# v and the heads' results kept in DRAM in a two-stage attention kernel, their projections done a tile at a time

## The chip, the cores and the metric

One NeuronCore of a Trainium2 chip runs the kernel. The metric is the device time of one execution in microseconds; lower is better. The core has four engines that compute and that wait for each other through semaphores: TensorE (PE) for matmuls, VectorE (DVE), ScalarE (ACT) and GpSimd (POOL). A fifth, SyncE (SP), issues the DMA transfers of this kernel in order. Each engine works through its own instructions strictly in the order in which they stand.

## What is computed

x is [8, 1024, 512], the context [8, 1024, 384], all float32. Two layers follow each other, each with a gate tanh(g) and a residual:

```
x = x + tanh(g0) * xattn(layernorm(x), ctx)
x = x + tanh(g1) * ffn(layernorm(x))

xattn: q = x Wq, k = ctx Wk, v = ctx Wv            (8 heads of 64)
       out = softmax(q k^T / sqrt(64)) v Wo + bo
ffn:   q, k, v = x W^T + b                          (16 heads of 32)
       q = (q / |q| + emb) * softplus(temp)
       h = softmax(q k^T / sqrt(32)) v
       gates = softmax over 15 routed (top 3 kept, times 3) and over 2 shared logits of h
       out = (h * sum of gates) Wp^T + bp
```

Where the projections need more than one rounded product they are made of two parts: a tensor is split into a rounded half (hi) and the rest (lo), and three products hi*hi, hi*lo, lo*hi are added.

## The kernel before, in words

The kernel runs two stages, first the cross attention of all eight batches, then the second attention of all eight. A batch is a *turn* of 64 *steps*. A step T takes 128 keys against 512 queries for one *group* of G heads that fill 128 channels (G is 2 in the first stage and 4 in the second). Eight steps make a *half*: all 1,024 keys for 512 queries. Two halves are a group, four groups a turn.

Each piece of work is an item with a short name: S the scores of one head in a step (line 963), ex its exponential on ACT (line 1168), ad the adding up of exponentials over a half on POOL (line 856), PV the weighing of v (line 978), sm the sums over partitions by a matmul with ones (line 990), sma their reciprocal on ACT, ev the normalizing multiply on DVE (lines 1352 to 1355). Exponentials lie in a ring of 7 (first stage) or 10 buffers (second); a step that is the first of a half writes to buffers of its own, onto which POOL adds the others. In the second stage POOL adds six of the eight steps of a half, four heads each.

For the next group, pq and pk project queries and keys, sd copies them six times a head into the operand stack (line 765), mx and mxr find the maxima (lines 945 and 1327), mt, ml and md put them there too (line 780). In the second stage ss, ssa, s2, s3 and s3p normalize the queries (lines 921, 1109 to 1123, 1309 to 1311, 843).

Around the change: vp is the value projection of one 128-row tile (8 tiles in a batch, 9 matmuls each in the first stage, 12 in the second); vpe copies it into v inside the SBUF tensor vh, which holds v of a whole batch (lines 1135 and 1319). cp copies the accumulator of a half out of PSUM into the same tensor (line 1173), over parts of v that are used up. When all heads of a batch are done, hs and hsl split a tile of 128 rows (lines 1196 and 1345), op is its output projection with 12 matmuls, xb and ope add bias, gate and residual, st stores it. gt makes the gates' logits of a tile (line 999) and gm the gates of four tiles (from line 1362). Because v and results share vh, the value projection of a batch stands in that batch's first steps, right after the output projection of the batch before.

What stands when is decided by class Plan before anything is recorded. Every item has an engine, a duration, a due step (numbers in the table AT) and items that it waits for. `run` plays them in time: each engine takes the ready item with the earliest due step. The outcome is one list, and every engine records its items in that list's order:

```
self.add(("vp", TT * j + t, k), "pe", 0.69, b0 + t - 0.4 + 0.4 * k / whole, ...)
self.add(("op", t, k), "pe", 0.69, b + 0.2 + 0.1 * k, ...)
for it in sorted(line, key=lambda x: (step[x], str(x))):
```

PSUM has eight banks. A unit of work takes one of them when it begins (mx takes four) and frees it when its taker has read it.

## Time and profile before

| | us |
|---|---|
| median of 3 runs | 5062.16 (5056.38 to 5085.25) |
| the profiled execution, time | 5047.21 |
| its span | 5045.4 |
| PE busy | 4586.3 |
| POOL busy | 3357.6 |
| DVE busy | 2949.3 |
| ACT busy | 2596.8 |

Busy time is the union of an engine's instructions. A matmul's end is modelled and matmuls overlap, so the pace of PE is better read from one start to the next. The time of an execution lies 2 us above the span of its instructions.

### The profile page before, as it was taken

Reading aid. Unit: us, or ns where it says so; the run is one execution under the profiler, and the core shown is the slowest. Engines: PE = TensorE matmul, PEld = TensorE weight load, DVE = VectorE, ACT = ScalarE, POOL = GpSimd, SP = SyncE. Lnnn points to the kernel's source line nnn. Section 1 sums busy time; section 2 is a strip of 40 time slices with the busy share of each in tenths; the row PEclk is TensorE's granted clock in tenths of the full one; section 3 lists DMA queues with packets and bytes.
Section 4 is the critical chain, followed back from the end, with each engine's and each line's share of the span. In section 5 each row is a group of like instructions: output and inputs, shape, how many; then the busy total and the mean of one; then the engine's idle time right before and its main releaser. Section 6 shows DMA issues by size and latency. Waiting matters only on the chain.

```text
span 5045.4 us, 66897 instructions
## 1 busy us (share of the span) xinstructions
PE 4586.3 (91%) x21568; PEld 2358.1 (47%) x21568; DVE 2949.3 (58%) x3955; ACT 2596.8 (51%) x4705; POOL 3357.6 (67%) x2667
## 2 busy tenths in 40 slices
PE   4999999999999999988988888988888988989988
PEld 3554555555555555453444444543543533534534
DVE  5464646464545464656656656656656666666562
ACT  3445444444444444546646546556456466466464
POOL 2656566666666565648768668678478578578597
PEclk8999999999999999999999899999899999999998
DMA  7344444353434343322332222313213222232320
GB/s 240 101 136 114 125 123 126 119 132 120 109 121 109 119 111 113 89 94 70 86 88 59 76 84 59 105 55 84 84 51 84 84 68 68 84 84 60 101 51 26
DMA packets 285207, 481.06 MB, mean 95 GB/s; under 512 B 32832, under 2 KB 165440, under 8 KB 275648
## 3 DMA queue, kind: packets, MB, share of 16 engines
q1 hardware_dynamic: 284864, 476.79, 34.5%
q8 instruction: 178, 2.92, 0.3%
q14 instruction: 165, 1.35, 0.1%
HBM read 223.14 MB, written 50.33 MB: 54 GB/s over the span
## 4 chain that ended last, share of the span: by engine, by line
PE 38%; issue 8%; ACT 5%; POOL 4%; DVE 4%; DMA 2%; SPq 0%; ACTq 0%; POOLq 0%; DVEq 0%
PE aux L877 13%; PE aux L978 9%; PE aux L963 8%; POOL added_f L856 4%; PE aux L945 3%; ACT probs L1168 2%; PE aux L990 2%; DVE nm L1327 1%; DMA xs<-x_after_xattn 1%; PE aux L999 1%; PE aux L921 1%; ACT more L1168 1%; DMA out<-xs 1%; DVE halves_f L1345 1%; DVE st L1263 1%
## 5 line engine op out<-in xcount | busy, mean ns | idle before, releaser
L856 POOL TENSOR_TENSOR added<-added,probs 128x512 f32<-128x512 f32 x1433 | 1802.5, 1291 | 921.6 <-PE aux L978 657.1
L1327 DVE TENSOR_REDUCE nm<-aux 128x2 f32<-128x1024 f32 x1536 | 1810.4, 1220 | 791.4 <-PE aux L945 789.5
L1168 ACT ACTIVATE probs<-aux 128x512 f32<-128x512 f32 x2151 | 1190.5, 600 | 904.8 <-PE aux L963 837.3
L963 PE MATMUL aux<-stack 128*128 128x512 f32 x4096 | 1426.0, 440 | 127.7 <-ACT probs L1168 78.7
L963 PEld LDWEIGHTS aux<-stack 128*128 128x128 f32 x4096 | 711.6, 192 | 973.7 <-issue 365.1
L978 PE MATMUL aux<-probs,vh 128*32 128x512 f32 (+1 forms) x4302 | 991.0, 632 | 66.2 <-ACT vh L1135 21.0
L856 POOL TENSOR_TENSOR added_f<-added_f,probs 128x512 f32<-128x512 f32 x537 | 677.4, 1295 | 184.0 <-PE aux L978 131.1
L945 PE MATMUL aux<-ck_hi,cq_hi 32*128 32x512 f32 (+1 forms) x3072 | 460.8, 492 | 158.2 <-DVE nm L1327 109.4
L877 PE MATMUL aux<-xT_hi,wqk 128*128 128x512 f32 x1536 | 583.2, 416 | 4.1 <-DVE xT_lo L1290 2.0
L945 PEld LDWEIGHTS aux<-ck_hi,cq_hi 32*128 32x128 f32 (+1 forms) x3072 | 182.9, 188 | 633.1 <-issue 618.2
L1168 ACT ACTIVATE more<-aux 128x512 f32<-128x512 f32 x537 | 302.3, 602 | 149.9 <-PE aux L963 111.0
L877 PEld LDWEIGHTS aux<-xT_hi,wqk 128*128 128x128 f32 x1536 | 293.9, 191 | 129.1 <-issue 67.1
L856 POOL TENSOR_TENSOR added_f<-added_f,more 128x512 f32<-128x512 f32 x231 | 292.7, 1293 | 51.7 <-PE aux L978 26.0
L856 POOL TENSOR_TENSOR added<-added,more 128x512 f32<-128x512 f32 x231 | 290.2, 1283 | 47.3 <-PE aux L978 39.9
L978 PEld LDWEIGHTS aux<-probs,vh 128*32 128x32 f32 (+1 forms) x4302 | 157.9, 120 | 347.4 <-issue 206.5
L978 PE MATMUL aux<-more,vh 128*32 128x512 f32 x1074 | 301.3, 640 | 12.9 <-ACT probs L1168 11.6
L877 PE MATMUL aux<-xT_lo,wqk 128*128 128x512 f32 x768 | 305.6, 398 | 0.0
L1352 DVE SCALAR_TENSOR_TENSOR aux<-aux,rn 128x512 f32<-128x512 f32 x128 | 88.9, 695 | 356.4 <-ACT rn L1181 200.0
L1168 ACT ACTIVATE added<-aux 128x512 f32<-128x512 f32 x256 | 145.2, 599 | 153.5 <-PE aux L963 152.6
L877 PE MATMUL aux<-wvo,halves_f 128*128 128x512 f32 x768 | 212.6, 427 | 0.0
L862 POOL TENSOR_TENSOR xs<-xs,bo_x 128x512 f32<-128x512 f32 x64 | 82.4, 1303 | 193.4 <-DMA xs<-in_x 193.3
L877 PE MATMUL aux<-wvo,halves_x 128*128 128x512 f32 x768 | 192.7, 398 | 2.0 <-DVE nm L1327 1.4
(132 smaller groups left out, 4800.9 us busy)
## 6 DMA issues: line engine op xcount, KB each, us to landing
wqk<-w_split SPq DMA_DIRECT2D x256, 256.0 KB, 3.8
wvo<-w_split SPq DMA_DIRECT2D x64, 1024.0 KB, 6.9
stack<-cq_hi SPq DMA_DIRECT2D x128, 256.0 KB, 5.1
stack<-ck_hi SPq DMA_DIRECT2D x128, 256.0 KB, 5.0
stack<-cq_hi SPq DMA_DIRECT2D x256, 128.0 KB, 2.3
stack<-ck_hi SPq DMA_DIRECT2D x256, 128.0 KB, 2.4
xs<-in_x SPq DMA_DIRECT2D x16, 1024.0 KB, 6.7
stack<-cq_lo SPq DMA_DIRECT2D x64, 256.0 KB, 4.9
```

Of the source, the lines that this page charges most:

```text
L856: pool.tensor_tensor(onto, onto, exp_buffer(T, e), ALU.add).then_inc(added_ok, 1)
L862: pool.tensor_tensor(xs[:, t % (TT // 2), :], xs[:, t % (TT // 2), :], bo[:], ALU.add).then_inc(biased, 1)
L877: ins = pe.matmul(out, lhs(a, k), rhs(c, k), start=k == 0 and i == 0, stop=k == whole - 1 and i == 2)
L921: done(it, pe.matmul(out, blk[:], sq[:, n], start=True, stop=True))
L945: ins = pe.matmul(aux[:, b, :], cq["hi"][r, t * P:(t + 1) * P], ck["hi"][r, half * HALF:(half + 1) * HALF], start=True, stop=True)
L963: ins = pe.matmul(out, stack[:, g % 2, e * ph.SLOTS + ks, jt * P:(jt + 1) * P], stack[:, g % 2, e * ph.SLOTS + qs, n * HALF:(n + 1) * HALF ...
L978: ins = pe.matmul(out[e * D:(e + 1) * D, :], v[:, g, jt * P + e * D:jt * P + (e + 1) * D], exp_buffer(T, e), start=jt == 0, stop=jt == TT - 1)
L990: ins = pe.matmul(out[e * D:(e + 1) * D, :], ones[:, 0:ph.SUM], exp_buffer(T, e), start=i == 0, stop=i == ph.APART)
L999: ins = pe.matmul(out[:, i * GC:(i + 1) * GC], outputs(t)[:, k, :], wg[:, k, :], start=k == 0, stop=k == NG - 1)
L1168: act.activation(exp_buffer(T, e), aux[:, o.bank["S", T, e], :], ACT.Exp, scale=ph.SCALE).then_inc(probs_ok, 1)
L1327: dve.tensor_reduce(nm[:, half, first:first + 2 * TT - t:TT], aux[:, b:b + 2, :], axis=AX.X, op=ALU.max, negate=True).then_inc(emptied["dv ...
L1352: link(dve.scalar_tensor_tensor(src, src, -1.0, rn[:], ALU.mult, ALU.mult))
```

## The change

v and the results of the heads no longer lie in SBUF for a whole batch. A tile of v goes from v_out to v_kept in DRAM (item vs), and a group's 128 channels of v come back before the group's first step (vl), into one of two buffers. After each half ev multiplies straight out of the accumulator's PSUM bank into h_raw (cp is gone), hs and hsl split that half, and hw stores both parts to h_kept. ol loads the two parts of one tile of 128 rows with all channels, into one of two buffers, for op. So the value projection of a batch can be done in the turn before it, and its output projection in the turn after it. In the second stage gt and ga add the gates' logits group by group into an SBUF tensor glog, and gm works there. The table AT has new numbers, the durations of the items are changed a little, POOL's adds are items of one head each, and `run` adds 0.1 to a PE item where the split of the array changes or PE was idle. The context comes in three loads of one chunk instead of two.

```diff
-AT = (dict(p=[2.5, 16.43, 38.3, 52.31], over=6.61, mx0=-7.25, mxn=10.51, ctx=[-6.39, 14.17, 26.21, 32.42], load=[12.79, 23.3], norm=[17.14, 36.41], turned=[20.42, 27.54], out=[62.76, 53.38], xr=40.63, split=37.96, off={"gt": 0.84, "ope": 1.44, "mxr": -0.41, "pkl": -3.12, "s3": -1.53, "s2": 0.03, "pqa": 1.84}),
-      dict(p=[1.88, 20.24, 30.77, 50.7], over=6.36, mx0=-4.19, mxn=11.61, load=[-5.48, 6.89], norm=[5.16, 26.23], turned=[24.2, 36.67], out=[61.26, 62.43], xr=52.33, off={"cp": -2.01, "hsl": -0.72, "s2": 0.05, "gt": -0.98, "s3": -0.06, "ev": 1.12, "PV": -0.81}))
+AT = (dict(p=[2.5, 18.6, 35.2, 51.9], over=7.4, mx0=-6, mxn=9, ctx=[19, 24, 29], load=[25, 32], norm=[28.5, 34.5], turned=[30.5, 37],
+           vp=[38, 3], out=[1.5, 3], xr=-8, split=42, off={}),
+      dict(p=[2, 18.6, 36, 50], over=6.5, mx0=-5.5, mxn=9, load=[25, 32], norm=[28.5, 34.5], turned=[30.5, 37],
+           vp=[39, 3], out=[1.5, 3], xr=-8, off={}))
...
-            if ph.is_added(T):
-                self.add(("ad", T), "pool", 1.3 * G, T, [("ex", T, 0), ("ad", T - 1), ("PV", T - T % TT)])
+                self.add(("ex", T, e), "act", 0.48, T - 1 + 0.2 * e, after)
+                if ph.is_added(T):
+                    self.add(("ad", T, e), "pool", 1.24, T + 0.2 * e, [("ex", T, e), ("ad", T, e - 1), ("ad", T - 1, e), ("PV", T - T % TT)])
             after = [("ex", T, G - 1), ("PV", T - 1)]
-            if T % TURN < TT:
-                after += [("vpe", TT * j + T % TURN)]
-            self.add(("PV", T), "pe", 1.05, T + 0.9, after)
+            after += [("vl", T // STEPS)]
+            self.add(("PV", T), "pe", 0.86, T + 0.9, after)
             if jt == TT - 1:
-                b = T + 1 + ph.AT.get("sums", 0)
-                self.add(("cp", h), "act", 0.6, T + 0.95, [("PV", T), ("cp", h - 1)])
-                self.add(("sm", h), "pe", 0.9 * (1 + ph.APART), b, [("ad", T - ph.APART), ("ex", T, G - 1), ("sm", h - 1)])
-                self.add(("sma", h), "act", 1.3, b + 0.3, [("sm", h), ("ev", h - 1)])
-                self.add(("ev", h), "dve", 2.2, b + 0.6, [("sma", h), ("cp", h), ("ev", h - 1)])
+                b = T + 1
+                self.add(("sm", h), "pe", 0.86 * (1 + ph.APART), b, [("ad", T - ph.APART, G - 1), ("ex", T, G - 1), ("sm", h - 1)])
+                self.add(("sma", h), "act", 1.2, b + 0.3, [("sm", h), ("ev", h - 1)])
+                self.add(("ev", h), "dve", 2.07, b + 0.6, [("sma", h), ("PV", T), ("ev", h - 1), ("hw", h - 1)])
+                if ph.ffn:
+                    self.add(("gt", h), "pe", 0.45, b + 1, [("ev", h), ("fb", 0)])
+                    self.add(("ga", h), "dve", 0.2, b + 1.2, [("gt", h), ("gm", 2 * (h // HALVES - 1) + h % 2)])
+                self.add(("hs", h), "act", 0.55, b + 1, [("ev", h)])
+                self.add(("hsl", h), "dve", 0.6, b + 1.2, [("hs", h), ("gt", h)])
+                self.add(("hw", h), "sp", 1.3, b + 1.5, [("hsl", h)])
...
     def values(self, j):
...
-        ph, b0 = stage(j), TURN * j
+
+        ph, b0 = stage(j), TURN * (j - 1)
         whole = ph.chunks("vp")
-        source = [("trl", j, n, NG - 1) for n in range(2)] if ph.ffn else [("cxl", j, ph.KC - 1)]
-        freed = [(kind, TT * j - 1) for kind in ("hsl", "gt")] + ([("ws", w) for w in range(4)] if j == 0 else [])
-        self.add(("wv", j), "sp", 1.3, b0 - 2, [("op", TT * j - 1, NG - 1), ("ws", ph.W + 2)])
-        for t in range(TT):
+        freed = [("ws", w) for w in range(4)] if j == 0 else []
+        before = ("op", TT * (j - 1) - 1, NG - 1) if j > 1 else ("vp", TT - 1, whole - 1)
+        self.add(("wv", j), "sp", 1.3, b0 + ph.AT["vp"][0] - 4, [before] * (j > 0) + [("ws", ph.W + 2)] + [("fs", 4 * NG - 1)] * ph.ffn)
+        for i in range(TT):
+            t, b = TT * j + i, b0 + ph.AT["vp"][0] + i * ph.AT["vp"][1]
+            source = [("trl", j, i // (TT // 2), NG - 1)] if ph.ffn else [("cxl", j, ph.KC - 1)]
             for k in range(whole):
-                self.add(("vp", TT * j + t, k), "pe", 0.69, b0 + t - 0.4 + 0.4 * k / whole, [("vp", TT * j + t, k - 1)] if k else [("wv", j)] + source + freed)
-            self.add(("vpe", TT * j + t), "dve" if ph.ffn else "act", 0.7, b0 + t, [("vp", TT * j + t, whole - 1)] + freed + ([("fb", 0)] if ph.ffn else []))
-        self.add(("wo", j), "sp", 1.3, b0 + TT, [("vp", TT * j + TT - 1, whole - 1), ("ws", ph.W + 3)])
+                self.add(("vp", t, k), "pe", 0.685, b + 0.4 * k / whole, [("vp", t, k - 1)] if k else [("wv", j), ("vp", t - 1, whole - 1)] + source)
+            self.add(("vpe", t), "dve" if ph.ffn else "act", 0.6, b + 0.5, [("vp", t, whole - 1), ("vs", t - 1)] + freed + [("fb", 0)] * ph.ffn)
+            self.add(("vs", t), "sp", 0.65, b + 0.7, [("vpe", t)])
+        for g in range(NG * j, NG * (j + 1)):
+            self.add(("vl", g), "sp", 0.65, (g - 1) * STEPS + 0.5, [("vs", TT * j + TT - 1), ("PV", (g - 1) * STEPS - 1), ("vl", g - 1)])
 
     def finish(self, j):
 
-        ph, at, b0 = stage(j), stage(j).AT, TURN * j
-        slots = NSPLIT[ph.ffn]
+        ph, at, b0 = stage(j), stage(j).AT, TURN * (j + 1)
+        whole = stage(j + 1).chunks("vp")
+        last = [("vp", TT * (j + 2) - 1, whole - 1)] if j + 1 < 2 * B else [("op", TT * j - 1, NG - 1)]
+        self.add(("wo", j), "sp", 1.3, b0 + at["out"][0] - 4, last + [("ws", ph.W + 3)])
         self.add(("xr", j), "sp", 2.6, b0 + at["xr"], [("tr", j + 1, 1, NG - 1), ("st", TT * j - 1), ("fs", NG * j + NG - 1)])
+        if ph.ffn:
+            for half in range(2):
+                self.add(("gm", 2 * j + half), "dve", 4, b0 + (2 if half else -4), [("ga", HALVES * (j + 1) - 2 + half), ("ope", TT * j - 1)])
...
+            self.add(("ol", t), "sp", 0.65, b - 1, [("hw", HALVES * (j + 1) - 2 + half), ("op", t - 2, NG - 1)])
             for k in range(NG):
-                self.add(("op", t, k), "pe", 0.69, b + 0.2 + 0.1 * k, [("op", t, k - 1)] if k else [("hsl", t), ("wo", j), ("xb", t), ("op", t - 1, NG - 1)])
-            self.add(("ope", t), "dve", 0.8, b + 0.6, [("op", t, NG - 1), ("xb", t)] + ([("gm", 2 * j + half)] if ph.ffn else []))
+                self.add(("op", t, k), "pe", 0.685, b + 0.1 * k, [("op", t, k - 1)] if k else [("ol", t), ("wo", j), ("op", t - 1, NG - 1)])
+            self.add(("ope", t), "dve", 0.66, b + 0.6, [("op", t, NG - 1), ("xb", t)] + [("gm", 2 * j + half)] * ph.ffn)
...
+        h_raw = sb("h_raw", [P, HALF])
+        h_hi = sb("h_hi", [P, HALF], F32R)
+        v_out = sb("v_out", [P, DM])
+        v = sb("v", [P, 2, TT, P])
+        parts = sb("parts", [P, 2, 2, NG, P], F32R)
...
+        v_kept = nc.dram_tensor("v_kept", [2, NG, P, TT, P], F32).ap()
+        h_kept = nc.dram_tensor("h_kept", [2, TT, P, 2, NG, P], F32).ap()
...
+                    elif kind == "vs":
+                        j, t = divmod(g, TT)
+
+                        wait_emptied(sp, ("vp", g))
+                        if j >= 2 and t == 0:
+
+                            for i in range(2):
+                                sp.wait_ge(v_loaded[i], 16 * (NG // 2) * (j - 1))
+                        sp.dma_start(v_kept[j % 2, :, :, t, :].rearrange("g p c -> p g c"), v_out[:].rearrange("p (g c) -> p g c", g=NG)).then_inc(v_stored, 16)
+                    elif kind == "vl":
+                        j = g // NG
+
+                        sp.wait_ge(v_stored, 16 * TT * (j + 1))
+                        if g >= 2:
+
+                            sp.wait_ge(weighed, (g - 1) * STEPS)
+                        sp.dma_start(v[:, g % 2], v_kept[j % 2, g % NG]).then_inc(v_loaded[g % 2], 16)
+                    elif kind == "hw":
+                        j, h = divmod(g, HALVES)
+
+                        sp.wait_ge(h_lo_ok, g + 1)
+                        if j >= 2 and h < 2:
+
+                            for i in range(2):
+                                sp.wait_ge(h_loaded[i], 16 * (TT // 2) * (j - 1))
+                        for part, done in enumerate((h_hi[:].bitcast(F32), h_raw[:])):
+                            sp.dma_start(h_kept[j % 2, h % 2 * TT // 2:(h % 2 + 1) * TT // 2, :, part, h // 2, :].rearrange("t p c -> p t c"),
+                                         done.rearrange("p (t c) -> p t c", c=P)).then_inc(h_stored, 16)
+                    elif kind == "ol":
+                        j, t = divmod(g, TT)
+
+                        sp.wait_ge(h_stored, 32 * (HALVES * (j + 1) - 1 + t // (TT // 2)))
+                        if g >= 2:
+
+                            wait_full(sp, ("op", g - 2))
+                        sp.dma_start(parts[:, g % 2].bitcast(F32), h_kept[j % 2, t]).then_inc(h_loaded[g % 2], 16)
...
 
                         pe.wait_ge(probs_ok, ph.scores(T, G - 1))
-                        if T % TURN < TT:
-
-                            wait_emptied(pe, ("vp", T // TURN * TT + jt))
+                        if T % STEPS == 0:
+
+                            pe.wait_ge(v_loaded[T // STEPS % 2], 16 * (T // STEPS // 2 + 1))
                         out = bank(it)
                         for e in range(G):
...
-                            pe.wait_ge(h_lo_ok, t + 1)
-                        ins = product(bank(it), lambda a, k: hi_lo[a][:, k, :], lambda c, k: wvo[:, c, k].rearrange("p g c -> p (g c)"),
+                            pe.wait_ge(h_loaded[t % 2], 16 * (t // 2 + 1))
+                        ins = product(bank(it), lambda a, k: parts[:, t % 2, a, k, :], lambda c, k: wvo[:, c, k].rearrange("p g c -> p (g c)"),
                                       [c0], NG)
...
+                        h = it[1]
+
+                        wait_emptied(act, ("sm", h))
+                        act.activation(h_hi[:], h_raw[:], ACT.Copy).then_inc(h_hi_ok, 1)
...
                         link(dve.scalar_tensor_tensor(src, src, -1.0, rn[:], ALU.mult, ALU.mult))
-                        link(dve.scalar_tensor_tensor(src, src, 2.0, rn[:], ALU.add, ALU.mult))
-                        dve.wait_ge(copied, h + 1)
-                        dve.tensor_tensor(vh[:, h % HALVES, :], vh[:, h % HALVES, :], src, ALU.mult).then_inc(emptied["dve"], 1)
+                        link(dve.scalar_tensor_tensor(rn[:], src, 2.0, rn[:], ALU.add, ALU.mult))
+                        dve.wait_ge(weighed, (h + 1) * TT)
+                        if h:
+
+                            dve.wait_ge(h_stored, 32 * h)
+                        dve.tensor_tensor(h_raw[:], aux[:, o.bank["acc", h], :], rn[:], ALU.mult).then_inc(emptied["dve"], 1)
+                    elif kind == "ga":
+                        h = it[1]
+                        src = full(("gt", h))[:, 0:TT // 2 * GC].rearrange("p (t c) -> p t c", c=GC)
+                        before = bg[:] if h // 2 % NG == 0 else glog[:, h % 2]
+                        if h // 2 % NG:
+
+                            wait_emptied(dve, ("gt", h - 2))
+                        dve.tensor_tensor(glog[:, h % 2], src, before, ALU.add).then_inc(emptied["dve"], 1)
...
                     elif kind == "hsl":
-                        t = it[1]
-                        hi, lo = split_slot(t)
-
-                        dve.wait_ge(h_hi_ok, t + 1)
-                        dve.tensor_tensor(lo, outputs(t), hi.bitcast(F32), ALU.subtract).then_inc(h_lo_ok, 1)
+                        h = it[1]
+
+                        dve.wait_ge(h_hi_ok, h + 1)
+                        if ffn:
+
+                            wait_full(dve, ("gt", h))
+                        dve.tensor_tensor(h_raw[:].bitcast(F32R), h_raw[:], h_hi[:].bitcast(F32), ALU.subtract).then_inc(h_lo_ok, 1)
```

The order on the engines shows what the diff can't. PE before, the start of a second-stage turn (stack is a score, wg,vh the gates' logits, wvo,halves_f the output projection, xT,wqk a query or key projection):

```order
L963 MATMUL aux<-stack 128x512 x4
L999 MATMUL aux<-wg,vh 128x18 x16
L963 MATMUL aux<-stack 128x512
L877 MATMUL aux<-wvo,halves_f 128x512 x24
L963 MATMUL aux<-stack 128x512
L877 MATMUL aux<-wvo,halves_f 128x512 x24
L945 MATMUL aux<-ck_hi,cq_hi 128x512 x4
L877 MATMUL aux<-xT_hi,wqk 128x512
```

Four tiles of the output projection stand there with one score between them. PE in the change, same place (the last value tile of the batch that begins, then scores, the gates' logits, and the first weighing of the turn):

```order
L905 MATMUL aux<-wvo,xT_lo 128x512
L979 MATMUL aux<-ck_hi,cq_hi 128x512 [waits emptied_by_dve,hi_ok,qs_ok]
...
L1031 MATMUL aux<-wg,h_raw 128x18 [waits emptied_by_dve]
L1031 MATMUL aux<-wg,h_raw 128x18 x3
...
L979 MATMUL aux<-ck_hi,cq_hi 128x512 x3
L1011 MATMUL aux<-added,v 32x512 [waits probs_ok,v_loaded0]
L1011 MATMUL aux<-added,v 32x512 x3
L1011 MATMUL aux<-probs,v 32x512 [waits probs_ok]
L1011 MATMUL aux<-more,v 32x512 x3
```

The output projection is gone from here, and the first weighing now waits for a load. The queue SP in the change, same place (v_kept<-v_out is the store of the last value tile, h_kept the results of the last half, stack<- the copies of the next group):

```order
L738 DMA wvo<-w_split 128x2048 [waits aux_full]
L738 DMA wvo<-w_split 128x2048
L747 DMA v_kept<-v_out 128x4x128 [waits emptied_by_dve]
L765 DMA h_kept<-h_hi 128x4x128 [waits h_lo_ok]
L765 DMA h_kept<-h_raw 128x4x128
L794 DMA stack<-cq_hi 32x1024 [waits qlo_ok,emptied_by_dve,scored]
L794 DMA stack<-ck_hi 32x1024
L794 DMA stack<-cq_lo 32x1024
...
L794 DMA stack<-ck_lo 32x1024
L755 DMA v<-v_kept 128x1024 [waits weighed,v_stored]
```

The load for which the first weighing waits stands behind the results of the half before and behind six of the copies.

## Rows read from the trace of the kernel before

**Rows 1.** Page, part 1: busy us, share of the span, instructions.
```profile
PE 4586.3 (91%) x21568; PEld 2358.1 (47%) x21568; DVE 2949.3 (58%) x3955; ACT 2596.8 (51%) x4705; POOL 3357.6 (67%) x2667
```

**Rows 2.** Busy time by stage: window, length, engines, PEclk, DMA share, GB/s.
```profile
349.00:2132.00 1783.00, 1752.70 (x7319) 932.79 (x7317) 959.28 (x1277) 836.39 (x1493) 1103.99 (x860) 0.99 0.44 118
2132.00:5013.00 2881.00, 2532.57 (x13007) 1256.46 (x13007) 1787.00 (x2376) 1610.97 (x2955) 2077.18 (x1666) 0.95 0.27 74
```

**Rows 3.** The same for first steps of a first-stage turn; a second-stage turn cut.
```profile
1120.00:1186.00 66.00, 63.83 (x264) 42.58 (x260) 23.91 (x45) 23.48 (x42) 22.61 (x18) 0.97 0.45 141
...
2883.00:2975.00 92.00, 84.61 (x399) 55.47 (x399) 50.52 (x92) 32.89 (x62) 34.94 (x28) 0.94 0.32 99
2975.00:3239.00 264.00, 233.62 (x1261) 103.47 (x1257) 177.03 (x221) 172.10 (x316) 223.54 (x179) 0.97 0.27 70
```

**Rows 4.** Time line of PE, second stage: start, us, engine, line, matmuls.
```profile
2874.62 1.06 PE L978 MATMUL aux<-probs,vh 128*32 128x512 f32 x8
2875.62 0.96 PE L877 MATMUL aux<-wvo,halves_f 128*128 128x512 f32 x3
...
2876.65 1.53 PE L877 MATMUL aux<-wvo,halves_f 128*128 128x512 f32 x6
2878.01 0.61 PE L963 MATMUL aux<-stack 128*128 128x512 f32 x2
```

**Rows 5.** Time line of POOL, turn boundary of the second stage, idle before in brackets.
```profile
2848.72 6.21 POOL L856 TENSOR_TENSOR added_f<-added_f,probs 128x512 f32<-128x512 f32 x5
2854.89 3.69 POOL L856 TENSOR_TENSOR added_f<-added_f,more 128x512 f32<-128x512 f32 x3
2858.55 4.91 POOL L856 TENSOR_TENSOR added_f<-added_f,probs 128x512 f32<-128x512 f32 x4
2878.80 1.29 POOL L862 TENSOR_TENSOR xs<-xs,bo_f 128x512 f32<-128x512 f32 x1 [15.35 <-DMA xs<-x_after_xattn]
2891.59 2.53 POOL L862 TENSOR_TENSOR xs<-xs,bo_f 128x512 f32<-128x512 f32 x2 [11.50 <-DMA xs<-x_after_xattn]
2898.35 1.26 POOL L862 TENSOR_TENSOR xs<-xs,bo_f 128x512 f32<-128x512 f32 x1 [4.23 <-DMA xs<-x_after_xattn]
2932.08 2.51 POOL L856 TENSOR_TENSOR added<-added,more 128x512 f32<-128x512 f32 x2 [32.47 <-PE aux L978]
```

**Rows 6.** Time line of DVE, at two turn boundaries of the second stage.
```profile
2850.01 14.61 DVE L1345 TENSOR_TENSOR halves_f<-vh,halves_f 128x512 fp32r<-128x512 f32 x2
...
3580.10 14.66 DVE L1345 TENSOR_TENSOR halves_f<-vh,halves_f 128x512 fp32r<-128x512 f32 x2
```

**Rows 7.** Groups by line; one tile's instructions (ns min/median/max).
```profile
L1345 DVE TENSOR_TENSOR halves_f<-vh,halves_f 128x512 fp32r<-128x512 f32 x64 | 81.2, 1288 | 4.5 <-ACT halves_f L1196 4.2
...
L843 POOL TENSOR_TENSOR cq_lo<-qwork,cq_hi 128x512 fp32r<-128x512 f32 x64 | 82.1, 1283 | 103.5 <-ACT cq_hi L1123 103.5
...
L1111 ACT ACTIVATE qwork<-qwork 128x512 f32<-128x512 f32 x64 | 40.5, 633 | 2.0
...
L1345 DVE TENSOR_TENSOR halves_f<-vh,halves_f x64: 676/692/14059, 2489.3 to 5032.5; 128x512 fp32r<-128x512 f32 x64
```

**Rows 8.** DMA: queue, packets, MB, share; issues with KB and us to landing.
```profile
q1 hardware_dynamic: 284864, 476.79, 34.5%
...
w_split<-xs_parts SPq DMA_DIRECT2D x32, 256.0 KB, 2.4
...
raw<-in_ctxT SPq DMA_DIRECT2D x8, 512.0 KB, 8.3
```

**Rows 9.** Time line of the queue SP: issues to the stack, either stage.
```profile
1209.10 1.32 SPq L765 DMA_DIRECT2D stack<-cq_hi  x1
...
2879.31 0.59 SPq L765 DMA_DIRECT2D stack<-ck_hi  x1
```

**Rows 10.** Time lines of DVE and PE, end of the program.
```profile
5019.51 0.69 DVE L1355 TENSOR_TENSOR vh<-vh,aux 128x512 f32<-128x512 f32 x1
...
5027.06 12.84 PE L877 MATMUL aux<-wvo,halves_f 128*128 128x512 f32 x48
```

294 lines of the change are left out of this document (122 added, 172 removed).

## The prediction

> **What bounds the kernel now.** I read the page's busy shares first. TensorE (PE) is busy 91% of the span, GpSimd (POOL) 67%, VectorE (DVE) 58%, ScalarE (ACT) 51% [rows 1]. A share over the whole span mixes two stages, so the second view is the busy time by stage. A first-stage turn (one batch: 64 steps of 128 keys by 512 queries) takes 1783/7 = 255 us, and PE is busy 98% of it. A second-stage turn takes 2881/8 = 360 us; there PE is at 88% and POOL at 72% [rows 2]. So the first stage has nothing to give but PE's own work, and the second has two engines near their limit with gaps in both.
>
> The third view cuts one turn of each stage at its eighth step. In the second stage the first 8 steps take 92 us and POOL works 34.9 us of them. The other 56 steps take 264 us and POOL works 223.5 us, 85% [rows 3]. There POOL sets the pace: its adds of the exponentials follow each other at 5 in 6.21 us, 1.24 us each, 192 in a turn. POOL's own time line shows the 92 us from inside: it waits 15.35, 11.50, 4.23 and 32.47 us, 63.5 us together, before the next half's adds begin at 2932 us [rows 5]. PE meanwhile does the output projection of the finished batch, the value projection of the next and a query/key projection. One such matmul takes (2878.01 - 2876.65)/6 = 0.227 us, and the weighing of v for one step 1.00 us [rows 4]. The two projections that the change moves are 2 x 8 tiles x 12 matmuls = 192 matmuls, 43.6 us in a turn, nearly all within those 8 steps. In short: for 92 us PE is the bound and POOL starves; for 264 us POOL is the bound and PE has slack.
>
> **The change, part by part.** The work of PE is the same: the order has the same numbers of matmuls. What moves is when. (1) *Projections spread.* In the first stage the 16 tiles now stand some three steps apart, so that no run without a score is longer than 5.2 us. In the second they do not spread so well. By counts from the new order at 0.227 us a matmul and 1.00 us a weighing, four runs without a score are left in a turn: 13.5 us (with 6.6 us just ahead of it), 15.5, 20.4 and 20.0 us. Before there was one crowd of some 73 us of PE work at the turn's start and no run above 8.1 us elsewhere.
>
> What is a second-stage turn worth then? The lower end: POOL works all through at the 85% of the other steps: (34.9 + 223.5)/0.847 = 305 us. The upper end: POOL's 258.5 us of work, plus its ordinary gaps (264 - 223.5 = 40.5 us in 56 steps, 46 in 64), plus what each run starves it. The ring of exponentials has ten buffers, so at most ten adds, 12.4 us, stand ahead of POOL when a run begins; about 2 us go until the first score, exponential and add are through. That leaves 8, 5, 10 and 10 us, 33 together. Two more: the wait for v (3) 9 us and the shared operands (4) 4 us. 258.5 + 46 + 33 + 13 = 350 us. I take 340, near the upper end, because the runs stand in the order as it is; the 10 us off are gaps around the small runs of now, which the 46 us and the 33 us both count. Against 360: 8 x 20 = **-161 us**.
>
> (2) *First stage.* In the 8 crowded steps PE is busy 63.8 of 66 us [rows 3], so spreading can return at most 2.2 us: 8 x 2 = **-16 us**. PE changes 42 times more often between whole and split array in the whole program; a change costs about 0.1 us (a weighing is two passes of 0.43 us and takes 1.00 [rows 4]): **+4 us**.
>
> (3) *The way through DRAM.* The stores and loads of v and of the heads' results are 128 + 64 + 256 + 128 = 576 more issues, all on SP, and 192 MB beside the 477 MB of now; in proportion 34.5% of the DMA engines' time becomes some 48% [rows 8]. SP has room: an issue takes 0.6 to 1.3 us [rows 9]. What counts is who waits. PE waits for v at the first weighing of each group. In the first stage the last value tile stands at step 58 and its load has six steps: hidden. In the second stage the last tile stands one step into the turn itself. Behind the last query sum of squares come nine instructions of its normalizing on ACT, DVE and POOL, 0.6 to 1.3 us each with the hand-overs [rows 7], 7.5 us, twelve copies to the stack at 0.6 us (7.6), two weight loads (0.8), the v store (0.7), the results' store (1.3), six more copies (3.8), and the load of v, 0.7 us and about 5 us to land: 27 us in one queue. The order gives PE 18 us of other work there, so PE stands some 9 us, with everything behind it: the scores, and POOL's adds. For a landing of 512 KB the rows offer 2.4 us (256 KB, a store) and 8.3 us (512 KB, a load queued in company) [rows 8]; I take 5, between them, since this load has little company. At the start nothing can be weighed before all 8 value tiles went through the single buffer v_out, each 0.6 us of copy, 0.6 of issue and 2.4 of landing, 29 us, and came back in 5; PE has 22 us to do there: **+12 us**. At the end the results of the last half go out and in again: 11.4 us from their last multiply to the first projection, against 7 now, when the gates' matmuls fill it, and with two buffers the last two tiles wait for a load each [rows 10]: **+6 us**.
>
> (4) *DVE and POOL.* The split of a result (result minus its rounded half) reads two SBUF operands. Now most such instructions fall where POOL is idle; still the mean is 1.288 us against a median of 0.692 [rows 7], 38 us too much over 64. Two of 14 us make 27 of them: the pair at 2850.01 takes 14.61 us while POOL puts through twelve adds without a pause, and the one at 3580 is like it [rows 6, 5]. In the change all 128 stand in the middle of the adds, and the gates' small sums move from PSUM to SBUF too. The Trainium skill (SBUF — State Buffer, section "Who interferes with whom") says that such a DVE instruction and a GpSimd one hold the shared ports one at a time for a whole instruction. By that rule each split would wait for one add at most; the 14 us in the trace is eleven adds, so the rule bounds it too low. In the sum stand 8 splits of 0.5 us a turn. The copy of the accumulator (128 on ACT at 0.6 us) goes; ACT is half idle, so nothing comes back. The accumulator's PSUM bank is held instead until the last multiply, about 5 us longer in each half, with four banks for the maxima: from 0 to 1 us a half, within my 340.
>
> **Sum:** 5047.2 - 161 - 16 + 4 + 12 + 6 = 4892; I forecast **4890 us**. This is against the profiled execution (span 5045.4, time 5047.2), which lies 0.3% below the median of 5062.
>
> **The rivals.** *B, balance:* the second stage reaches POOL's own pace, because scores slip in earlier than the plan thought. For it: outside the boundary POOL keeps 85% now. Turn 318 instead of 340: 4892 - 8 x 22 = 4715. Chance 0.16. *C, only cut up:* the four runs and the wait for v starve POOL as much as the one stretch did. Four runs are 69 us of matmuls against 73. Turn 355 to 360: 5010 to 5060. Chance 0.12. *D, slower: the adds lock out the splits.* 64 splits of the second stage, and nine small two-operand sums in each of 16 gate passes, meet POOL at full work. The other 62 splits of now lost 11 us together, at most 1.2 each, so at least nine of them met an add: 2 of some 12 were caught. While DVE stands, the maxima stand, PE stops at their banks, and after POOL's queue of adds is empty POOL stops as well. At that rate 10 of 64 are caught: +130 us if nothing hides it; beyond 12 the whole gain is gone, at 20 the time is 4892 + 20 x 13 = 5150. For it: the 14 us. Against: a backlog of eleven adds is rare, and while it lasts POOL, the bound, is working. Chance 0.20. *E: the change does not do what it says,* since SP works in order: loads of v or of the results, stuck behind copies to the stack, hold PE at every group. 128 boundaries at 2 us: 5150. Chance 0.04. The skill's same page ("A bandwidth-pool intuition that's wrong (but worth ruling out)") holds HBM for the usual bottleneck, which would speak against any way through DRAM; the profile moves 118 and 74 GB/s by DMA in the two stages at shares of 0.44 and 0.27 [rows 2], so I give that no chance of its own.
>
> **The numbers.** My forecast has 0.48 and covers 4800 to 4990; B reaches down to 4715, D up to 5150. The range 4730 to 5110 leaves out half of B and half of D. A measurement of this kernel can tell about 0.5%. Faster by more: my case, B, a little of C: 0.66. Within: most of C: 0.11. Slower: D and E: 0.23.
>
> **What would show it.** Right: POOL's longest wait in a second-stage turn falls from 32 us to under 22, its turns last 330 to 350 us, first-stage turns 250 to 256 us, and the wait before the first weighing of a turn names the load of v with about 9 us. (4) shows in the mean of the splits: above 2.5 us is D. Wrong: a first-stage turn above 260 us (copies to the stack slowed by the added traffic), or ACT waiting for them; POOL busy over 85% of the second stage is B.

## The result

The changed kernel takes 5229.9 us (median of 4 runs, 5215.9 to 5245.7) against 5059.3 for the kernel before on the same chip: a ratio of 1.033, 95% interval 1.028 to 1.037. It is **slower by 3.3%**; the forecast was 4890. The profiled execution has a span of 5223.1 us, 178 more than before.

The page of the changed kernel, part 1, answers to [rows 1]. PE has as much to do as before; VectorE (DVE) has 248 us more.

```profile
PE 4624.4 (89%) x21568; PEld 2369.0 (45%) x21568; DVE 3197.2 (61%) x3955; ACT 2534.5 (49%) x4577; POOL 3378.0 (65%) x2667
```

Busy time by stage answers to [rows 2], with the first turn ahead and what follows the last weighing behind (window; length; PE, PEld, DVE, ACT, POOL; PEclk, DMA share, GB/s):

```profile
25.00:394.00 369.00, 290.63 (x1179) 161.03 (x1179) 184.08 (x241) 137.52 (x243) 155.21 (x119) 0.90 0.57 162
394.00:2212.00 1818.00, 1776.77 (x7388) 940.11 (x7388) 999.09 (x1299) 800.52 (x1432) 1123.62 (x863) 0.99 0.60 164
2212.00:5179.00 2967.00, 2531.24 (x12896) 1250.07 (x12895) 1993.86 (x2359) 1586.38 (x2889) 2070.13 (x1657) 0.92 0.38 105
5179.00:5223.00 44.00, 25.75 (x111) 17.81 (x109) 12.15 (x32) 2.12 (x4) 12.25 (x10) 0.83 0.47 154
```

Cut in the same way, before has 324, 1783, 2881 and 32 us. So the start lost 45 us, the first stage 35, the second 86 and the end 12. The second stage, which was to gain 161 us, has turns of 371 us in place of 360.

Where DVE's 248 us are, its groups by line show: the split, which answers to the first row of [rows 7], takes 2986 ns in the mean where the second stage's took 1288. All 128 take 382.2 us in place of 141.3. By tile, the shortest is 681 ns and the longest 35.5 us.

```profile
L1355 DVE TENSOR_TENSOR h_raw<-h_raw,h_hi 128x512 fp32r<-128x512 f32 x128 | 382.2, 2986 | 41.0 <-ACT h_hi L1208 40.8
...
L1355 DVE TENSOR_TENSOR h_raw<-h_raw,h_hi x128: 681/1396/35512, 185.4 to 5193.2; 128x512 fp32r<-128x512 f32 x128
```

PE's waits, the whole span (what it waited for: us, times, longest), say who pays. The maxima's matmul (L979) waits for DVE to read the last ones' banks. That was 109.4 us before.

```profile
PE aux L979 <- DVE nm L1335: 241.6, 123, 13.8
PE aux L997 <- ACT probs L1195: 81.5, 143, 2.5
PE aux L997 <- ACT qb L1136: 46.7, 7, 6.8
PE aux L925 <- ACT xs L1103: 41.6, 2, 27.3
PE aux L1011 <- DMA v<-v_kept: 38.1, 8, 27.3
```

One such place in the second stage, from the time lines of DVE, POOL and PE:

```profile
3074.05 0.22 DVE L1376 TENSOR_TENSOR glog<-aux,bg 128x72 f32<-128x72 f32 x1
3074.19 12.18 DVE L1355 TENSOR_TENSOR h_raw<-h_raw,h_hi 128x512 fp32r<-128x512 f32 x1
3086.29 4.67 DVE L1335 TENSOR_REDUCE nm<-aux 128x2 f32<-128x1024 f32 x4
...
3073.50 8.66 POOL L884 TENSOR_TENSOR added<-added,probs 128x512 f32<-128x512 f32 x7
3082.11 3.71 POOL L884 TENSOR_TENSOR added<-added,more 128x512 f32<-128x512 f32 x3
3094.55 1.28 POOL L884 TENSOR_TENSOR added<-added,probs 128x512 f32<-128x512 f32 x1 [8.73 <-ACT probs L1195]
...
3078.02 0.49 PE L997 MATMUL aux<-stack 128*128 128x512 f32 x1
3087.76 0.80 PE L979 MATMUL aux<-ck_hi,cq_hi 32*128 32x512 f32 x4 [9.24 <-DVE nm L1335]
```

The split starts at 3074.2 and ends at 3086.4, 0.6 us after POOL's last add of the run (3085.8). Ten adds end while it stands: it is *caught*, the word used from here on. The read of the maxima is queued behind it on DVE, PE stands 9.24 us for that read, and POOL, which had its run, then stands 8.73 us for exponentials of scores that PE had not made. That is the loss in small: both engines that matter stop, one after the other. Splits of over 2.5 us are 23 in all, 19 of them in the second stage. Each of the 19 ends 0.55 us after the last add before a pause of POOL of 3.1 us or more. The second stage's 64 splits take 284 us together, 240 more than 64 of the shortest.

Not every split that meets an add stands so long. Of the same 64, 34 more took 0.95 to 1.84 us. They slip in between two adds that follow each other without a pause, and the next add then takes 1.74 us in place of 1.28, as the second of these three does (DVE and POOL):

```profile
3134.85 1.27 DVE L1355 TENSOR_TENSOR h_raw<-h_raw,h_hi 128x512 fp32r<-128x512 f32 x1
...
3134.29 4.20 POOL L884 TENSOR_TENSOR added_f<-added_f,more 128x512 f32<-128x512 f32 x3
```

What decides between the two stays open. In both cases the exponentials of the next add had been ready for 0.9 us or more.

A stop of PE also costs clock, for which the forecast had no term. From 3078 to 3088 us, where PE stands, the granted clock of TensorE is 0.66, and 0.58 in the 4 us behind: most of that at the lower of its two levels, 1.2 GHz. Twelve matmuls of the output projection take 4.19 us there, 0.35 each, where the prediction has 0.227 from [rows 4]. Over the second stage the clock is 0.92 where it was 0.95.

### The profile page after: what moved, and what is told of

It reads as the page before. It is cut to its first block, busy times and chain, and to the rows that moved or that the text cites. A ratio compares the mean times of both kernels' runs of the same rounds, so it can differ in the third digit from the quotient of the medians.

```text
span 5223.1 us, 67382 instructions
## 1 busy us (share of the span) xinstructions
PE 4624.4 (89%) x21568; PEld 2369.0 (45%) x21568; DVE 3197.2 (61%) x3955; ACT 2534.5 (49%) x4577; POOL 3378.0 (65%) x2667
## 3 DMA queue, kind: packets, MB, share of 16 engines
q1 hardware_dynamic: 515824, 678.18, 46.7%
## 4 chain that ended last, share of the span: by engine, by line
PE 67%; DVE 14%; DMA 6%; issue 5%; ACT 3%; SPq 3%; POOL 2%; ACTq 0%; DVEq 0%; POOLq 0%
PE aux L905 23%; PE aux L997 16%; PE aux L1011 15%; DVE nm L1335 6%; PE aux L979 6%; DVE h_raw L1355 5%; PE aux L1023 3%; SPq L794 2%; ACT probs L1195 1%; DMA stack<-ck_lo 1%; PE aux L949 1%; DMA out<-xs 1%; POOL added L884 1%; PE aux L925 1%; PE aux L1031 1%
## 5 line engine op out<-in xcount | busy, mean ns | idle before, releaser
L884 POOL TENSOR_TENSOR added<-added,probs 128x512 f32<-128x512 f32 x1433 | 1822.7, 1304 | 1078.5 <-PE aux L1011 720.1
L997 PE MATMUL aux<-stack 128*128 128x512 f32 x4096 | 1456.2, 447 | 182.2 <-ACT probs L1195 81.5
L1011 PE MATMUL aux<-probs,v 128*32 128x512 f32 (+1 forms) x4302 | 1010.3, 646 | 0.0
L979 PE MATMUL aux<-ck_hi,cq_hi 32*128 32x512 f32 (+1 forms) x3072 | 469.2, 503 | 258.7 <-DVE nm L1335 241.6
L979 PEld LDWEIGHTS aux<-ck_hi,cq_hi 32*128 32x128 f32 (+1 forms) x3072 | 187.9, 193 | 707.4 <-issue 695.8
L905 PE MATMUL aux<-wvo,parts 128*128 128x512 f32 x1536 | 420.5, 418 | 11.9 <-issue 10.0
L1355 DVE TENSOR_TENSOR h_raw<-h_raw,h_hi 128x512 fp32r<-128x512 f32 x128 | 382.2, 2986 | 41.0 <-ACT h_hi L1208 40.8
L872 POOL TENSOR_TENSOR cq_lo<-qb,cq_hi 128x512 fp32r<-128x512 f32 x64 | 82.4, 1288 | 437.0 <-ACT cq_hi L1154 436.8
L905 PEld LDWEIGHTS aux<-wvo,parts 128*128 128x128 f32 x1536 | 304.0, 202 | 104.4 <-issue 38.5
L1011 PE MATMUL aux<-more,v 128*32 128x512 f32 x1074 | 313.0, 665 | 0.0
L1011 PEld LDWEIGHTS aux<-probs,v 128*32 128x32 f32 (+1 forms) x4302 | 162.7, 122 | 289.2 <-issue 223.4
```

The lines of the kernel that those rows point to most:

```text
L872: pool.tensor_tensor(cq["lo"][:, q], qb[:, n], cq["hi"][:, q].bitcast(F32), ALU.subtract).then_inc(qlo_ok, 1)
L884: pool.tensor_tensor(onto, onto, exp_buffer(T, e), ALU.add).then_inc(added_ok, 1)
L905: ins = pe.matmul(out, lhs(a, k), rhs(c, k), start=k == 0 and i == 0, stop=k == whole - 1 and i == 2)
L979: ins = pe.matmul(aux[:, b, :], cq["hi"][r, t * P:(t + 1) * P], ck["hi"][r, half * HALF:(half + 1) * HALF], start=True, stop=True)
L997: ins = pe.matmul(out, stack[:, g % 2, e * ph.SLOTS + ks, jt * P:(jt + 1) * P], stack[:, g % 2, e * ph.SLOTS + qs, n * HALF:(n + 1) * HALF ...
L1011: ins = pe.matmul(out[e * D:(e + 1) * D, :], v[:, T // STEPS % 2, jt, e * D:(e + 1) * D], exp_buffer(T, e), start=jt == 0, stop=jt == TT - 1)
```

## The experiments

**Theory L**: what is lost are DVE's instructions with two SBUF operands, caught behind GpSimd's adds. **Rival M**: the transfers through DRAM. **Rival Q**: the queue of SyncE, which works in order. Each run is timed beside the kernel before on its chip; ratios are to that, with their 95% interval. "A turn" is the mean of seven turns, from windows like those above: for before 254.7 us in the first stage and 364.9 in the second (the last one, which is short, left out), for the change 259.7 and 375.9, with a first turn of 324 and 369. The chips differ from group to group, so where two versions ran on different chips their ratios say more than their times.

### Three ways round the split, and the bytes alone

**split_tiny**: one column of the split's 512. It leaves out the rest of the lower part.

```
- dve.tensor_tensor(h_raw[:].bitcast(F32R), h_raw[:], h_hi[:].bitcast(F32), ALU.subtract)
+ dve.tensor_tensor(h_raw[:, 0:1].bitcast(F32R), h_raw[:, 0:1], h_hi[:, 0:1].bitcast(F32), ALU.subtract)
```

> Leaves out the lower part of the heads' results, all but one column of it: the split on VectorE becomes a subtraction of 1 column in place of 512, in the same place of the same order. Theory L (the split, which reads two SBUF operands, is caught behind GpSimd's adds, and what stands behind it on VectorE, the reading of the maxima's banks, then holds PE): VectorE loses some 375 of its 382 us there, a middle turn of the second stage falls from 363-378 to 335-345, the wait of the maxima's matmul for VectorE from 204 us in the second stage to under 120, the whole to 4980-5040. Rival M (the transfers through DRAM take the time: DMA share 0.44 to 0.60 in the first stage): the time stays above 5180. Rival Q (the stores of the heads' results wait on the sync queue and hold what is behind them): also above 5180, unless the wait is that for the split itself, and then the wait for the maxima stays at 204 us.

Measured: 5177.4 us, ratio 1.022 (1.017 to 1.026), far from L's 4980 to 5040 and just under the 5180 of M and Q. What failed is a premise, that a split of one column is no longer caught. Its splits, by tile (ns min/median/max):

```profile
L1355 DVE TENSOR_TENSOR h_raw<-h_raw,h_hi x128: 146/857/34972, 180.9 to 5140.0; 128x1 fp32r<-128x1 f32 x128
```

With one column they still take 227.7 us together, thirteen of them 5 to 35 us. The time is the wait, and making the instruction small does not take the wait away. So this run parts L from M and Q less than it was meant to.

**split_on_pool**: the same six lines moved from DVE's program to GpSimd's, same place in the order.

```
- dve.tensor_tensor(h_raw[:].bitcast(F32R), h_raw[:], h_hi[:].bitcast(F32), ALU.subtract).then_inc(h_lo_ok, 1)
+ pool.tensor_tensor(h_raw[:].bitcast(F32R), h_raw[:], h_hi[:].bitcast(F32), ALU.subtract).then_inc(h_lo_ok, 1)
```

> The same subtraction of 512 columns, in the same place of the same order, by GpSimd in place of VectorE. Theory L: nothing on VectorE can wait for GpSimd any more; GpSimd takes 128 more instructions of some 1.24 us, 10 us a turn, and its adds come that much later. A middle turn of the second stage 342-355, the whole 5020-5110. Rivals M and Q: 5200 or more, since transfers and the order of the sync queue are the same and GpSimd has more work.

Measured: 5138.9, ratio 1.014 (1.009 to 1.020): 91 us faster than the change, although GpSimd has more to do. Turns 256.9 and 369.3, not 342 to 355. M and Q cannot have the whole loss, nor have the splits. DVE's groups say where the rest went: with the splits gone, other instructions with two SBUF operands are caught, the minimum over the maxima (16 or 32 columns) and the gates' subtraction (60 columns).

```profile
L1348 DVE TENSOR_TENSOR nm<-nm 128x16 f32<-128x16 f32 (+1 forms) x64 | 79.0, 1234 | 2.1
L1385 DVE TENSOR_TENSOR glog<-glog,gm 128x60 f32<-128x60 f32 x16 | 42.9, 2682 | 0.5
```

**split_from_psum**: the last multiply stays in the bank, ScalarE copies out of it, and the bank's taker is the split.

```
- "PV": "ev"}
+ "PV": "hsl"}
- dve.tensor_tensor(h_raw[:], aux[:, o.bank["acc", h], :], rn[:], ALU.mult)
+ dve.tensor_tensor(acc, acc, rn[:], ALU.mult)
- dve.tensor_tensor(h_raw[:].bitcast(F32R), h_raw[:], h_hi[:].bitcast(F32), ALU.subtract)
+ dve.tensor_tensor(h_raw[:].bitcast(F32R), aux[:, o.bank["acc", h], :], h_hi[:].bitcast(F32), ALU.subtract)
```

> The heads' results stay in their PSUM bank, where the last multiply is done in place; ScalarE copies them out, and the split reads one PSUM and one SBUF operand. Each bank is held some 2 us longer, and the plan's order moves a little with it. Theory L: the split takes 0.65 to 0.8 us each instead of 2.99, none is caught, a middle turn of the second stage 342-352, the whole 5000-5080. Rivals M and Q: 5200 or more.

Measured: 5165.3, ratio 1.019 (1.015 to 1.023). The form is free of catches, as expected:

```profile
L1361 DVE TENSOR_TENSOR h_raw<-aux,h_hi 128x512 fp32r<-128x512 f32 x128 | 87.6, 684 | 38.0 <-ACT h_hi L1214 38.0
```

But turns are 256.3 and 372.4, not 342 to 352. Part of the rest is again the minimum and the gates (49.3 and 46.9 us).

**before_traffic**: the kernel before, and 48 stores of 256 KB a turn.

```
+ for _ in range({"sd": 2 - ffn, "md": 2 - ffn, "st": 2}.get(kind, 0) if batch(it) else 0):
+     sp.dma_start(spare[sent], bo_x[:]).then_inc(spared, 16)
```

> The kernel before with 48 more stores of 256 KB each a turn from the second turn on, from SBUF into a DRAM tensor that nobody reads: 12 MB a turn, what the change adds, and nothing else of it. Theory L: transfers as such cost next to nothing in the second stage; the first stage by 5 us a turn at most: 5060-5110 in all. Rival M: the added bytes alone give the greater part of the 170 us: 5150 or more, and the first stage's turns 258-262 instead of 253-256.

Measured: 5204.6, ratio 1.028 (1.022 to 1.034); turns 267.1 and 379.1. By this run M has the whole loss, and the expectation of L fails. But these stores stand directly ahead of the copies to the stack and the maxima's rows, and part of the second stage's cost is again L's: splits of 14 us are five here, against two in the kernel before. Two more runs part bytes from issues, and later ones show the change's own bytes.

**before_issues** and **before_bytes**: 48 stores of 2 KB at the same places, or 12 of 1 MB at a quarter of them.

```
+     sp.dma_start(spare[sent], bo_x[0:1, :]).then_inc(spared, 16)
...
+     sp.dma_start(spare[sent], bo_x[:].unsqueeze(1).to_broadcast([P, 4, DM])).then_inc(spared, 16)
```

> The kernel before with 48 more stores a turn from the second turn on, as in before_traffic, but of 2 KB each: the issues on the sync queue, without the bytes. Rival I (the queue's time counts, 0.66 us an issue): most of the 134 us of before_traffic, 5150-5200, with the first stage's turns at 262-270. Rival B (the bytes count): 5060-5090, first stage's turns 253-256.

> The kernel before with 12 more stores of 1 MB each a turn from the second turn on: the bytes of before_traffic with a quarter of its issues. Rival B: 5150-5230, the first stage's turns at 262-275. Rival I: 5070-5110, the first stage's turns under 258.

Measured: 5085.1, ratio 1.000 (0.996 to 1.004), turns 255.9 and 363.4; and 5137.8, ratio 1.013 (1.009 to 1.018), turns 261.1 and 369.3. Issues alone cost nothing that shows in the time. The bytes cost 6.4 and 4.4 us a turn; in 48 pieces 12.4 and 14.3, so the two together cost more than their sum.

### The other instructions with two SBUF operands

**no_locks**: split_from_psum, and

```
- dve.tensor_tensor(nm[:, 0, 0:G * TT], nm[:, 0, 0:G * TT], nm[:, 1, 0:G * TT], ALU.min)
+ dve.tensor_reduce(least[:, 0:G * TT], nm[:, :, 0:G * TT].rearrange("p a t -> p t a"), axis=AX.X, op=ALU.min)
- dve.tensor_tensor(lg[:, :, 0:NE], lg[:, :, 0:NE], gm[:, :, 0:1].to_broadcast([P, TT // 2, NE]), ALU.subtract)
+ ins = dve.tensor_scalar(lg[:, t, c], lg[:, t, c], gm[:, t, i:i + 1], None, ALU.subtract)
```

> split_from_psum, and the two small VectorE instructions that were caught in its place read one SBUF operand: the minimum over the two halves of the maxima is one reduction over a strided view, and the gates' subtraction of their maximum takes a column as its scalar. Same plan and order as split_from_psum. Theory L2 (what is left of the second stage's loss is these catches, 29 us and 43 us beyond their shortest in split_from_psum): the catches over 2 us are gone, the wait of the maxima's matmul for VectorE falls under 100 us, and the second stage loses 40-80 us: turns 366-372, whole 5090-5125. Rival P (the plan's turn of 340 is out of reach for another reason, the transfers or the queue that issues them): turns stay at 374-379, whole 5150-5170.

**no_locks_start**: the plan lets the third group's weights, the second group's copies and the next v weights go behind the stores of v.

```
+ [("vs", TT - 1)] * (g == 2)      (wl)
+ [("vl", 0)] * (g == 1)           (sd)
+ [("vl", 1)] * (j == 1)           (wv)
```

> no_locks, and at the start of the program the eight stores of v and its first load are issued ahead of the third group's weights, the second group's copies and the next batch's v weights (2 MB), on the same queue. Theory: the first turn's 360 us fall to 338-345 (the stores then go round in some 4 us each where the last one took 12 us), nothing else changes: 15-20 us faster than no_locks. Rival: the second group's copies then come late, and the time is as no_locks within 5 us.

Measured: 5120.1, ratio 1.006 (1.003 to 1.009), turns 255.1 and 369.1, as expected; and 5101.3, ratio 1.005 (1.002 to 1.008), turns 255.6 and 368.9. The first stage is now where it was before the change, 255 us a turn at a DMA share of 0.61: **the change's own bytes cost the first stage nothing that shows**. (What the spreading gave back there, 2 us a turn at most by the prediction, could hide as much.) Of its 5 us a turn the splits had 3.4 and the minimum 1.2. The first turn falls from 361 to 334 us by the order of the queue alone (windows of the first turn, no_locks_start behind):

```profile
25.00:386.00 361.00, 287.32 (x1182) 159.19 (x1183) 175.09 (x242) 137.77 (x243) 154.40 (x120) 0.89 0.59 166
```

```profile
25.00:359.00 334.00, 284.71 (x1181) 157.50 (x1181) 175.26 (x241) 137.69 (x243) 154.19 (x119) 0.92 0.63 180
```

In the changed kernel the last two stores of v went out at 138.8 and 151.3 us, since the first of them, issued behind copies and 2 MB of weights, landed only at 150.6. The loads followed at 153.7 (time line of SP, the two stores in one row; PE's wait at that place):

```profile
138.78 12.93 SPq L747 DMA_DIRECT2D v_kept<-v_out  x2
153.65 0.81 SPq L755 DMA_DIRECT2D v<-v_kept  x2
...
PE aux L1011 <- DMA v<-v_kept: 27.3, 1, 27.3
```

The second stage did not get near 340: the subtraction with a column as its scalar is caught too. Here is what it does, on DVE, POOL, ACT and PE of no_locks_start:

```profile
3941.08 8.77 DVE L1392 TENSOR_SCALAR glog<-glog,gm 128x15 f32<-128x15 f32 x8
...
3941.51 7.38 POOL L885 TENSOR_TENSOR added_f<-added_f,probs 128x512 f32<-128x512 f32 x6
3950.71 1.27 POOL L885 TENSOR_TENSOR added_f<-added_f,probs 128x512 f32<-128x512 f32 x1 [1.82 <-ACT probs L1196]
...
3949.89 0.26 ACT L1218 ACTIVATE gexp<-glog 128x72 f32<-128x72 f32 x1 [8.93 <-DVE glog L1392]
3950.06 0.58 ACT L1196 ACTIVATE probs<-aux 128x512 f32<-128x512 f32 x1
...
3950.69 1.28 PE L998 MATMUL aux<-stack 128*128 128x512 f32 x2 [8.04 <-ACT probs L1196]
```

A circle: the first of the eight, 15 columns on DVE, waits 7.8 us for the adds to pause; ACT's exponential of the gates waits for DVE, the exponentials of the scores stand behind it, PE waits for those, and the adds pause only when they have used up the exponentials there are.

**gates_on_act**: no_locks_start, with the subtraction as ScalarE's bias.

```
- dve.tensor_scalar(lg[:, t, c], lg[:, t, c], gm[:, t, i:i + 1], None, ALU.subtract)
+ act.activation(gexp[:, t, c], glog[:, it[1] % 2, t, c], ACT.Exp, bias=gm[:, t, i:i + 1])
```

> no_locks_start, and the gates' subtraction of their maximum goes into ScalarE's exponentials as a bias (8 activations of some 0.25 us a half turn), so that VectorE has no instruction there that reads two SBUF operands ahead of them. Theory C (a circle: VectorE's first subtraction of 15 columns waits 7.8 us for GpSimd's adds to pause, ScalarE's exponential of the gates waits for it, the scores' exponentials stand behind that one on ScalarE, and the adds only pause when they run out of exponentials; one such stop of 8 us a turn): the PE gap of 8 us some 60 us ahead of each turn's end is gone, turns of the second stage 364-368 instead of 372-376, 45-60 us faster than no_locks_start, 5040-5060. Rival: GpSimd's adds were what bounds that stretch and PE only waits later: turns stay at 370 or more.

Measured: 5133.4, ratio 1.017 (1.014 to 1.020): 32 us **slower** than no_locks_start (1.2% by the ratios), turns 374.0 in place of 368.9, where 45 to 60 us faster was expected. The stop of 8 us is gone and a longer one stands in its place. DVE and POOL:

```profile
3201.90 17.32 DVE L1401 TENSOR_TENSOR g<-gsum,g 128x4 f32<-128x4 f32 x1
3219.15 0.15 DVE L1402 TENSOR_TENSOR g<-gexp,g 128x4 f32<-128x4 f32 x1
...
3197.11 8.69 POOL L885 TENSOR_TENSOR added_f<-added_f,probs 128x512 f32<-128x512 f32 x7
3205.76 3.69 POOL L885 TENSOR_TENSOR added_f<-added_f,more 128x512 f32<-128x512 f32 x3
3209.43 8.56 POOL L885 TENSOR_TENSOR added_f<-added_f,probs 128x512 f32<-128x512 f32 x7
3217.96 1.25 POOL L885 TENSOR_TENSOR added_f<-added_f,more 128x512 f32<-128x512 f32 x1
```

Four columns, 0.16 us of work, stand 17.3 us while fifteen adds end. Eight of the sixteen gate passes have such a stop, of 17.1 to 22.9 us. ACT is no longer held, so the adds have more to eat and pause later. Freeing one instruction hands the wait to the next with that form, and it may be longer there.

### The places

**v_first**, **vp_early**: gates_on_act, and

```
+ last += [("vl", NG * (j + 1))] * (j + 1 < 2 * B)      (the output weights behind the first load of v)
...
- vp=[39, 3]
+ vp=[36, 2.8]                                          (vp_early only, second stage)
```

> gates_on_act, and the 2 MB of output weights at a turn's start are issued behind the first load of v instead of just ahead of it. Theory: that load landed 9.5 us after its issue behind those weights, where a load of its size takes 3 to 5 us, and PE waited 8.6 us for it in seven turns; with it ahead the wait falls to 3-4 us: another 30-40 us in all, second-stage turns some 5 us shorter. Rival: the weights then come late and PE waits for them at the output projection, no gain within 10 us.

> v_first, and the table places the second stage's v projection from step 36 of a turn, every 2.8 steps, in place of step 39, every 3. Theory: PE no longer waits for v at a turn's start at all, and what it does in the turn's last steps is spread; second-stage turns 350-358, whole 4950-5010, below the kernel before. Rival: the banks and the adds of steps 44 and 60 set the turn, and it stays at 360 or more, whole 5000 or more.

Measured: 5100.6, ratio 1.004 (1.000 to 1.007); and 4987.8, ratio 0.981 (0.974 to 0.988). v_first takes 11 us off a second-stage turn (363.1), more than expected, and adds 7 to each first-stage turn (261.7); all_fixed below, with the old order of the weights in the first stage, is back at 255.0. With the earlier places a second-stage turn is 350.0. Not all of these 13 us are the places: of seven catches of 17 us in v_first's second stage four of 12 to 23 us are left.

**before_plan**: the kernel before, its plan with the new durations, delays and tiling cost; one of some thirty lines:

```
- self.add(("PV", T), "pe", 1.05, T + 0.9, after)
+ self.add(("PV", T), "pe", 0.86, T + 0.9, after)
```

> The kernel before with the changed kernel's durations, delays and the cost of a change of tiling in its plan, and nothing else of the change: this part alone. Theory of the prediction (better durations make a better order): second-stage turns 355-360 instead of 363, first stage +-3 a turn, whole 5030-5060. Rival: the order is no better on the chip, since its losses are waits that the plan doesn't know (VectorE behind GpSimd's adds): within 0.5%, or slower where a new instruction is caught.

Measured: 5017.2, ratio 0.987 (0.978 to 0.995); turns 256.4 and 358.0. This part of the change, alone, is a gain of 1.3%. The two splits of 14 us are gone in it, and how much of the gain that is no run tells.

**after_vp**: the changed kernel with vp=[36, 2.8] and nothing else. **after_order**: that, with no_locks_start's three lines and v_first's line for the second stage alone.

> The changed kernel with one place of its table changed, the second stage's v projection from step 36 every 2.8 steps in place of 39 every 3; all splits on VectorE as they were. Theory P (the places cost the second stage most, since PE waits for v and the last steps of a turn are crowded): turns of 355-362, whole 5070-5130. Theory L (the catches cost most): turns of 370 or more, whole above 5180.

> after_vp, and at the start the stores and the first load of v ahead of the other copies, and in the second stage the output weights behind the first load of v. Theory P: first turn 340-345 in place of 369, second-stage turns 350-358, whole 5010-5070. Theory L: whole above 5130.

Measured: 5233.2, ratio 1.028 (1.020 to 1.036), turns 257.0 and 377.0; and 5186.1, ratio 1.019 (1.012 to 1.027), a first turn of 336, turns 258.6 and 376.1. With the catches left in, better places give the second stage nothing. P is out as the cause of the loss.

**all_fixed**: vp_early with v_first's line for the second stage alone. **adds_pause**: that, and GpSimd waits for the gates' sums (DVE copies one column onto itself to signal it).

```
+ elif kind == "gm":
+     pool.wait_ge(gates_done, it[1] + 1 - 2 * B)
```

> vp_early with the output weights behind the first load of v in the second stage alone. Theory: vp_early's first-stage turns of 260 were that order (the weights late for the projection), and go back to 253: 50 us faster than vp_early, 4925-4960, second stage unchanged at 348-352. Against after_order it has the splits without a second SBUF operand: the difference of the two is what the catches cost once the places are right, 60-100 us by L, under 40 by P.

> all_fixed, and GpSimd waits, at the gates' sums' place in the order, until VectorE has done them (twice a turn in the second stage). Theory: the sums of four columns are no longer caught for 12 to 23 us; GpSimd stands some 3 to 6 us each time, which its share of 77% allows; turns 344-350, 0 to 40 us faster. Rival: what GpSimd loses comes back at the turn's crowded steps, where the scores wait for the adds: 0 to 40 us slower.

Measured: 4945.4, ratio 0.972 (0.965 to 0.978), turns 255.0 and 349.3; and **4912.2, ratio 0.965 (0.957 to 0.973)**, turns 255.1 and 345.7, the fastest version of the study. Making the busiest engine but PE wait is a gain: no DVE instruction of either stage takes over 2.5 us any more, where all_fixed had two of 12 and 14 us. Against before_plan (0.987), the part that needs no way through DRAM, it is 2% faster.

**splits_back**: adds_pause, the split's first operand `h_raw[:] if ffn else aux[:, o.bank["acc", h], :]`.

> adds_pause with one operand changed: in the second stage the split reads the copy of the heads' result in SBUF (ScalarE makes it anyway, for the gates) in place of the same values in the PSUM bank. Same order, same banks, same waits, same columns. Theory L: the 64 splits are caught again, some 20 of them for 5 to 14 us, 150 us or more beyond their 0.68 in all, turns go from 345 to 370-378, the whole from 4912 to 5080-5160. Rival P: the gain came with the changed order, the splits are caught but it costs under 60 us.

Measured: 4962.7, ratio 0.975 (0.971 to 0.980): 50 us for 64 operands, under a third of what was expected. By tile:

```profile
L1368 DVE TENSOR_TENSOR h_raw<-h_raw,h_hi x64: 681/1412/20846, 2213.5 to 4923.8; 128x512 fp32r<-128x512 f32 x64
```

Only two are long, 11.2 and 20.8 us, both in the last turn; the others took 1.9 us at most, and most of them slipped in between two adds. So what a form costs hangs on where the order puts it, and after_order and all_fixed differ in the order too.

**same_order**: after_order, plan, order and banks untouched. Splits on GpSimd as in split_on_pool, minimum and gates as in all_fixed, GpSimd's wait as in adds_pause.

> after_order with its plan, order and banks untouched; the splits go to GpSimd in their place of the order, the maxima's minimum is one reduction, the gates' subtraction is ScalarE's bias, and GpSimd waits for the gates' sums. Theory L: no catch is left; GpSimd carries 10 us a turn more; second-stage turns 350-360 in place of 378, whole 4980-5060 against 5186. Rival O (the order and its banks lose the time, whatever the forms): turns stay at 368 or more, whole 5110 or more.

Measured: 4952.3, ratio 0.978 (0.973 to 0.983), against after_order 234 us less, or 4.1% by the ratios, some 208 us. The second stage of after_order, and of same_order, seven turns:

```profile
2171.00:4804.00 2633.00, 2266.06 (x11526) 1131.91 (x11525) 1808.48 (x2154) 1408.76 (x2572) 1822.25 (x1459) 0.92 0.38 106
```

```profile
2145.00:4585.00 2440.00, 2216.10 (x11524) 1101.96 (x11523) 1538.08 (x2084) 1432.14 (x2663) 1881.61 (x1516) 0.96 0.41 114
```

In the same order DVE has 270 us less and GpSimd 59 us more, and a turn falls from 376.1 to 348.6. Some 38 of the 270 us are the work of the 56 moved splits, the rest is wait. PE's busy time falls by 50 us for as many matmuls, at a clock of 0.96 in place of 0.92. L is shown: in that order the catches, with the clock that they cost, are worth 208 to 234 us, and Rival O is out.

## Why the prediction was wrong

**The step that failed is in (4)**, "in the sum stand 8 splits of 0.5 us a turn", and with it the sign. These 4 us a turn were 27.5 between after_order and same_order. Nineteen of the second stage's splits stood over 2.5 us, and 34 more about one add. Rival D had the mechanism, the place and the direction (at 20 caught it gave 5150; measured 5230), and what was to show it, a mean above 2.5 us, came at 2.99. It had a chance of 0.20. The second stage came 247 us above the forecast, where D has 20 x 13 = 260; the first stage with 47 and the start with 33 are the rest of the way to 5230, and D left them at the forecast. Two arguments held it down. "A backlog of eleven adds is rare": seven to eleven adds went past at least one split in every turn of the second stage, and 29 once. And "while it lasts POOL, the bound, is working": it does, and then stands, as the 8.73 us above show; the adds done in the run were done early, and the scores for the next were not made.

**(1) Projections spread** was right as far as it can be read without the catches. The 340 us are an eighth of the whole stage, against 360. Cut so, up to the end of the last weighing, same_order has 343.6 us and vp_early 343.1, so most of the 10 us taken off the upper end of 350 were there. (By the mean of seven turns they are 348.6 and 350.0, against 364.9 before.) Their orders differ from the change's by the places of one projection and a few transfers, vp_early's also by the longer hold of the accumulator's bank. No run has the change's own places without catches and without its wait for v. As planned, POOL's longest pauses in a turn fell, from mostly 30.0 to 32.5 us to 25.6 to 27.7 in the change (not "under 22"), and to 9.2 to 10.1 in same_order. Part of what (1) sees is not the spreading at all: before_plan has 6.9 us a turn of it from the plan's numbers.

**(2) First stage:** -12 us were forecast, +35 measured. With neither the split nor the minimum reading two SBUF operands on DVE it is 1783 to 1789 us (v_first and vp_early apart), as before: no net gain, no loss. The 16 us of the spreading and the 4 us of the changes of the array have no run of their own. The forecast left out that the first stage, too, has its adds: the 63 splits up to its end took 97 us, where 63 of the shortest take 43.

**(3) Start:** +12 forecast, +45 measured. The 29 us of the store chain were counted as if the queue were free; the last stores stood behind copies and weights, and one of them took 11.9 us to land. The forms give 8 us of it back and the order of the queue 27; then +10 is left. **Wait for v:** 9 us forecast; in the change 1.5 us a turn show, since PE is held elsewhere first, and in no_locks_start it is there with 8.0 to 9.7 us in seven turns. The reason was partly another: not SP's queue but 2 MB of output weights issued 2.7 us ahead of the load. The landing of a load of v is 5.2 us in the median (5 taken), 9.5 us behind those weights. **End:** +6 forecast, +12 measured. **Bytes and issues** cost the first stage nothing that shows, as forecast. Its DMA share is 0.60; the queue's over all is 46.7%, against "some 48%". (The 192 MB are 201 of the page's MB.)

**The skill's rule** (the Trainium skill, SBUF — State Buffer, section "Who interferes with whom"), that the shared pair is held for one whole instruction and the other engine fully blocks, agrees in kind: 128 splits with one operand in PSUM never took over 0.693 us, 64 reductions over a strided view took 0.205 in the mean, and a `tensor_scalar` of 15 columns was caught, which the page allows that form. For 34 of the second stage's splits it holds in size too: DVE's turn comes after one add, and the next add is held up by half a microsecond. For the other 19 it is too mild, as the prediction said: the turn came after 10 adds in the place shown, and after 15 in gates_on_act.

## What to carry to other kernels

Where GpSimd runs one SBUF instruction after another, give VectorE no instruction with two SBUF operands, however small, nor a `tensor_scalar` over SBUF like the one caught here: read one from PSUM, fold the operation into a ScalarE bias or a reduction, or let GpSimd wait at that place. Where such an instruction will be caught can't be told from its form alone; measure the longest, not the mean. Look for the whole class at once, since the next one takes over the wait of the one removed. And a gap on the busiest engine is not explained by its queue being full before it: look who stood while it ran.

## What was not expected of the hardware

- The wait does not hang on the size of the caught instruction: 512 columns 12.2 us, 15 columns 7.8, 4 columns 17.3, 1 column up to 35.0.
- A long wait (over 2.5 us in the second stage) ends with a pause of GpSimd; a short one ends between two adds that follow each other without one. If the caught instruction holds up, by way of others, what feeds GpSimd, that makes the pause; if not, the wait is longer (7.8 against 17.3 us at the same place of a turn).
- 12 MB more a turn cost a first-stage turn from nothing (the change's own, half of it loads, DMA share 0.61) to 12.4 us (as 48 stores just ahead of the copies to the stack, share 0.55). So the share alone does not tell the cost. That the place in the queue decides is likely; no run changes the place alone.
- Why 48 pieces of 256 KB cost two to three times what 12 of 1 MB do, when 48 of 2 KB cost nothing, stays open. So does why the splits of adds_pause's order nearly all wait for one add at most when they read two SBUF operands again, and those of the change's order do not.
